# Mixture-of-experts stage on one Trainium2 core: two experts per matrix product on row halves, scaling on GpSimd, halves added by TensorE

## The reference, cut to what matters

```python
shared = jnp.zeros_like(h)
for s in range(shared_w.shape[0]):          # two shared experts
    shared = shared + _gelu(_c1(feats, shared_w[s], shared_b[s])) / shared_w.shape[0]
...
vals, idx = jax.lax.top_k(scores, TOP_K)    # TOP_K = 4
wts = jax.nn.softmax(vals / TEMPERATURE, axis=1)
gate_w = jnp.zeros((B, NUM_EXPERTS), x.dtype).at[jnp.arange(B)[:, None], idx].add(wts)
out = shared
for e in range(NUM_EXPERTS):
    out = out + _gelu(_c1(feats, expert_w[e], expert_b[e])) * gate_w[:, e][:, None, None, None]
return out + residual
```

## Time and profile before

| | us |
|---|---|
| median of 3 runs (lowest, highest) | 7360.36 (7358.43, 7375.71) |
| the profiled execution, its own time | 7338.2 |
| its span in the trace | 7336.4 |
| PE busy over the span | 6420.7 (88%) |
| DVE busy | 5526.3 (75%) |
| ACT busy | 3980.0 (54%) |
| POOL busy | 3924.6 (53%) |

### The profile page before, as it was taken

The page is one execution under the profiler, slowest core; times in us unless marked ns, Lnnn a source line. Parts: engine busy times, 40 slices in busy tenths (PEclk is TensorE's granted clock), DMA queues, the critical chain, the costliest instruction groups (busy, mean ns, idle before and its releaser), DMA issues. The chain is left out here.

```text
span 7336.4 us, 119069 instructions
## 1 busy us (share of the span) xinstructions
PE 6420.7 (88%) x36560; PEld 3370.5 (46%) x36560; DVE 5526.3 (75%) x5048; ACT 3980.0 (54%) x6930; POOL 3924.6 (53%) x2716
## 2 busy tenths in 40 slices
PE   8968699999987369876999999999989999999991
PEld 7852233333345224565222222222247777777771
DVE  4654577777732358401899999999979999999996
ACT  5425366666631357401666767767645555555552
POOL 0100122222210300000899999999979999999991
PEclk9989799999988689857999999999979999999995
DMA  2243233343345623444222222222220000000006
GB/s 72 71 163 143 59 99 97 99 101 99 100 119 125 249 103 103 128 104 73 39 41 38 39 40 37 40 40 37 34 63 11 10 9 9 10 10 9 9 7 187
DMA packets 638484, 518.35 MB, mean 71 GB/s; under 512 B 250045, under 2 KB 569315, under 8 KB 629627
## 3 DMA queue, kind: packets, MB, share of 16 engines
q1 hardware_dynamic: 636667, 507.10, 28.0%
q10 hardware_dynamic: 1600, 8.52, 0.5%
HBM read 304.91 MB, written 171.32 MB: 65 GB/s over the span
## 5 line engine op out<-in xcount | busy, mean ns | idle before, releaser
L2605 DVE TENSOR_TENSOR_SCAN spa_hs<-spa_p_d,spa_hs,spa_bx 128x967 f32<-128x967 f32 x584 | 1346.5, 2306 | 1.2 <-ACT spa_p_d L2504 1.1
L2311 POOL TENSOR_TENSOR spa_hc<-spa_hs,spa_cr 128x966 f32<-128x966 f32 x592 | 1313.8, 2239 | 44.4 <-DVE spa_hs L2605 40.2
L2759 POOL TENSOR_TENSOR spe_hc<-spe_hs,spe_bcu 128x1024 f32<-128x1024 f32 x520 | 1218.2, 2359 | 67.2 <-DVE spe_hs L2971 66.2
L2971 DVE TENSOR_TENSOR_SCAN spe_hs<-spe_p_d,spe_bx 128x1024 f32<-128x1024 f32 x520 | 1161.6, 2276 | 36.3 <-ACT spe_p_d L2919 33.0
L2846 PEld LDWEIGHTS spe_p_y<-spe_idt,spe_hc 128*128 128x128 f32 x8320 | 966.1, 192 | 143.8 <-issue 143.8
L1065 DVE TENSOR_REDUCE attention_nm<-attention_p_s 128x2 f32<-128x640 f32 x1024 | 789.1, 812 | 260.1 <-PE attention_p_s L922 259.0
L2846 PE MATMUL spe_p_y<-spe_idt,spe_hc 128*128 128x128 f32 x8320 | 979.2, 276 | 0.0
L1023 ACT ACTIVATE attention_pr<-attention_p_t 128x512 f32<-128x512 f32 x1280 | 712.0, 600 | 419.4 <-PE attention_p_t L945 287.2
L2504 ACT ACTIVATE spa_p_d<-spa_p_d,spa_av 128x483 f32<-128x483 f32 x1184 | 706.5, 636 | 376.3 <-PE spa_p_d L2375 376.3
L2919 ACT ACTIVATE spe_p_d<-spe_p_d 128x896 f32<-128x896 f32 x520 | 446.2, 902 | 758.7 <-PE spe_p_d L2829 758.4
L2375 PE MATMUL spa_p_d<-spa_du,spa_hot 32*128 32x483 f32 x2368 | 644.9, 620 | 12.8 <-DVE spa_hs L2605 3.3
(11 more groups left out here) (429 smaller groups left out, 10585.3 us busy)
## 6 DMA issues: line engine op xcount, KB each, us to landing
attention_qs<-scratch_qp SPq DMA_DIRECT2D x768, 64.0 KB, 2.8
spa_uc<-spa_du SPq DMA_DIRECT2D x148, 241.5 KB
attention_rc<-scratch_den SPq DMA_DIRECT2D x128, 256.0 KB
scratch_qp<-patch_parts SPq DMA_DIRECT2D x64, 384.0 KB, 2.3
spa_xt<-scratch_x SPq DMA_DIRECT2D x148, 121.5 KB, 2.7
front_xs<-in_x_dram SPq DMA_DIRECT2D x64, 256.0 KB, 3.0
scratch_xf<-front_out SPq DMA_DIRECT2D x128, 128.0 KB, 2.5
patch_x<-scratch_xf SPq DMA_DIRECT2D x8, 2048.0 KB, 18.8
```

What stands on the lines that cost most here:

```text
L2311: nc.gpsimd.tensor_tensor(hc[:, k % 8:k % 8 + 2, :], hs[:, k:k + 2, 0:NA], cr2[:, s % 2, :].unsqueeze(1).broadcast_to([128, 2, NA]), ALU.m ...
L2605: last = nc.vector.tensor_tensor_scan(joined(hs, j), p_d[j % 2][:, 511 - NA:512 + NA], joined(bx, j), hs[:, k, NA - 1:NA], ALU.mult, ALU.add)
L2759: nc.gpsimd.tensor_tensor(hc[:, k, :, d, :].rearrange("p s d t -> p d s t"), hs[:, k % 2, d, :, :], rows, ALU.mult)\
L2971: nc.vector.tensor_tensor_scan(hs[:, k % 2, d].rearrange("p d s t -> p (d s t)"), p_d[h][:, :], bx[:, k % 2, d].rearrange("p d s t -> p (d ...
```

## The change

What it does:

- **Products.** A product's weights are no longer 128 x 128 with two zero blocks. Two experts of one image stand side by side, 64 rows by 128 columns, and the product reads the 64 partitions of that image alone. So a chunk has three pairs k = 0, 1, 2 (first two chosen experts, the shared two, last two chosen), each of two products p = 0, 1 on the lower and upper row half, into banks `p_x[k][p]`: six banks. In a bank, partitions 0 to 63 hold one expert and 64 to 127 the other, all of one image. For that the shared weights `sw` and biases `sb` are laid out anew by the host.
- **Shared experts** (pair 1) are made one chunk ahead of the others. ACT writes their Gelu to SBUF (`gs`) and POOL multiplies by one half (`us`).
- **Sums.** DVE's `add_first` adds gate times pair 0 to `us` (into `acc`), `add_last` adds gate times pair 2. Then PE adds the two partition halves of `acc` with a 128 x 64 matrix `fold` of two identities (`add_halves`), images on different columns, into one of two banks `p_o`, and DVE's `finish` adds the residual.
- **Order.** The queues are written with `stream`, a helper that was there before: each part has a lag in chunks, so at step i the part with lag 1 works on chunk i - 1.
- **Building the weights.** Every second chosen expert's product with the selection is made by POOL; the reductions, now over all 128 partitions at once, stay on DVE: eight instead of sixteen.
- **Transfers.** 13 instead of 14 before the stream; `hot2` and `gx` gather every other expert's row. Four buffers for features instead of two. Chunks alternate between the two pairs of images.

The diff, cut (declarations, and the functions removed, which are shown above, are left out):

```diff
-def experts(nc, hr, feats, sel, wts, we, be, ws, bs, out1):
+def experts(nc, hr, feats, sel, wts, we, be, ws, bs, ident, out1):
...
+        def columns(s, r):
+
+            return bass.ds((r * 2 + s // 2) * 512, 512)
 
         @block.sync
...
+            with nc.allow_non_contiguous_dma(reason="every other expert's gate"):
+                for q in range(2):
                     r = slice(64 * q, 64 * q + 64)
...
+                    sp.dma_start(hot2[r], sel.rearrange("b (k q) e -> q (b k) e", q=2)[q:q + 1].broadcast_to([64, B * TOP // 2, NE]))\
+                        .then_inc(loaded, 16)
+                    sp.dma_start(gx[r].rearrange("p b k -> p (b k)"),
+                                 wts.rearrange("b (k q) -> q (b k)", q=2)[q:q + 1].broadcast_to([64, B * TOP // 2])).then_inc(loaded, 16)
+
+            def load(c, s, r):
+
+                after(sp, x_done, 4 * (c - 3))
+                sp.dma_start(fs[:, s, :], feats[:, s % 2, columns(s, r)]).then_inc(f_in[s], 16)
+
+            def store(c, s, r):
+                sp.wait_ge(out_ready, c + 1)
+                sp.dma_start(ov[:, s % 2, columns(s, r)], os[:, s % 2, :]).then_inc(stored[s % 2], 16)
+
+            stream(sp, NCH, UX, 2 * UX, 5, (0, load), (5, store))
...
+        @block.tensor
+        def _(pe):
+            def spread_shared(c, s, r):
+                pe.wait_ge(f_in[s], 16 * r + 16)
+                for p in range(2):
+
+                    after(pe, shared_active, 2 * c + (p - 1))
+                    rows = slice(64 * p, 64 * p + 64)
+                    nc.tensor.matmul(p_x[1][p][:, :], wsh[rows, :], fs[rows, s, :], start=True, stop=True).then_inc(shared_done, 1)
+
+            def spread(k, free):
+
+                def run(c, s, r):
+                    for p in range(2):
+
+                        after(pe, free, 2 * c + (p - 1))
+                        rows = slice(64 * p, 64 * p + 64)
+                        nc.tensor.matmul(p_x[k][p][:, :], wx[rows, s % 2, k // 2, :], fs[rows, s, :], start=True, stop=True).then_inc(x_done, 1)
+                return run
+
+            def add_halves(c, s, r):
+                after(pe, out_ready, c - 1)
+                for p in range(2):
+                    pe.wait_ge(last_added, 2 * c + (p + 1))
+                    mm = nc.tensor.matmul(p_o[s % 2][64 * p:64 * p + 64, :], fold[:, :], acc[:, s % 2, p, :], start=True, stop=True)
+                mm.then_inc(folded, 1)
...
+            stream(pe, NCH, UX, UX, 2, (1, spread(0, first_added)), (0, spread_shared), (1, spread(2, last_added)), (2, add_halves))
 
         @block.scalar
         def _(act):
...
+            stream(act, NCH, UX, UX, 1, (1, activate(0, first_active)), (0, activate_shared), (1, activate(2, last_active)))
 
         @block.vector
         def _(dve):
...
+            def choose(a, k, t):
+                nc.vector.tensor_reduce(wx[:, a, k // 2, C * (k % 2):C * (k % 2) + C], pk[:, t], AX.X, ALU.add).then_inc(w_ready, 1)
...
+            def add_first(c, s, r):
+                t, b = s % 2, lambda p: 2 * (s % 2) + p
+                for p in range(2):
+                    dve.wait_ge(first_active, 2 * c + (p + 1))
+                    dve.wait_ge(shared_scaled, 2 * c + (p + 1))
+
+                    after(dve, folded, c - 1)
+                    nc.vector.scalar_tensor_tensor(acc[:, t, p, :], p_x[0][p][:, :], gx[:, b(p), 0:1], us[:, t, p, :], ALU.mult,
+                                                   ALU.add).then_inc(first_added, 1)
+
+            def add_last(c, s, r):
+                t, b = s % 2, lambda p: 2 * (s % 2) + p
+                for p in range(2):
+                    dve.wait_ge(last_active, 2 * c + (p + 1))
+                    dve.wait_ge(first_added, 2 * c + (p + 1))
+                    nc.vector.scalar_tensor_tensor(acc[:, t, p, :], p_x[2][p][:, :], gx[:, b(p), 1:2], acc[:, t, p, :], ALU.mult,
+                                                   ALU.add).then_inc(last_added, 1)
+
+            def finish(c, s, r):
+                dve.wait_ge(folded, c + 1)
+
+                after(dve, stored[s % 2], 16 * (r * 2 + s // 2))
+                nc.vector.tensor_tensor(os[:, s % 2, :], p_o[s % 2][:, :], hr[:, s % 2, columns(s, r)], ALU.add).then_inc(out_ready, 1)
+
+            stream(dve, NCH, UX, UX, 2, (1, add_first), (2, finish), (1, add_last))
+
+        @block.gpsimd
+        def _(pool):
+            def scale(c, s, r):
+                for p in range(2):
+                    pool.wait_ge(shared_active, 2 * c + (p + 1))
+
+                    after(pool, first_added, 2 * c + (p - 3))
+                    nc.gpsimd.tensor_tensor(us[:, s % 2, p, :], gs[:, s % 2, p, :], share[:, :], ALU.mult).then_inc(shared_scaled, 1)
...
+            stream(pool, NCH, UX, UX, 0, (0, scale))
```

More of the change, by code:

```diff
@@ L66, in turns, with after, stream, fixed @@
     return run
+def after(eng, sem, n):
+    if not (isinstance(n, int) and n <= 0):
+        eng.wait_ge(sem, n)
+def stream(eng, n, unroll, head, tail, *parts):
+    def fixed(i):
+        for lag, part in parts:
+            c = i - lag
+            if 0 <= c < n:
+                part(c, c % unroll, c // unroll)
+    for i in range(head):
+        fixed(i)
+    with eng.Fori(0, (n - head) // unroll - 1) as j:
+        for s in range(unroll):
+            for lag, part in parts:
+                c = head + s - lag
+                part(j * unroll + c, c % unroll, j + c // unroll)
+    for i in range(n - unroll, n + tail):
+        fixed(i)
 KH = H // 2
@@ new lines, in experts @@
+        gx = st.sb("gx", [128, B, TOP // 2])
+        idt = st.sb("idt", [128, 128])
+        fold = st.sb("fold", [128, C])
+        share = st.sb("share", [128, 512])
+        fs = st.sb("fs", [128, UX, 512])
+        gs = st.sb("gs", [128, 2, 2, 512])
+        us = st.sb("us", [128, 2, 2, 512])
+        acc = st.sb("acc", [128, 2, 2, 512])
+        os = st.sb("os", [128, 2, 512])
+        p_x = [[st.ps(f"p_x{k}{p}", [128, 512]) for p in range(2)] for k in range(NP)]
+        p_o = [st.ps(f"p_o{s}", [128, 512]) for s in range(2)]
@@ L1885, in _, with activate_shared @@
-        @block.tensor
-        def _(pe):
-            pe.wait_ge(w_ready, 1)
-            for a in range(2):
-                @turns(pe, N)
-                def _(j):
-                    for s in range(2):
-                        n = a * N * 2 + 2 * j + s
-                        pe.wait_ge(f_in[s], 16 * (a * N + j) + 16)
-                        for k in range(NX):
-                            pe.wait_ge(summed[k], n)
-                            mm = nc.tensor.matmul(p_x[k][:, :], wx[:, a, k, :], fs[:, s, :], start=True, stop=True)
-                            mm.then_inc(x_done, 1)
+            def activate_shared(c, s, r):
+                for p in range(2):
+                    act.wait_ge(shared_done, 2 * c + (p + 1))
+                    after(act, shared_scaled, 2 * c + (p - 3))
+                    nc.scalar.activation(gs[:, s % 2, p, :], p_x[1][p][:, :], ACT.Gelu, bias=bsh[:, 0:1]).then_inc(shared_active, 1)
@@ L2081 @@
 TD = TK * DE
-def after(eng, sem, n):
-    if not (isinstance(n, int) and n <= 0):
-        eng.wait_ge(sem, n)
 RA = 7
```

160 lines of the change are left out of this document (57 added, 103 removed).

## The result

| | before | after |
|---|---|---|
| median, us (lowest, highest) | 7359.4 (7355.06, 7375.71) | 7414.78 (7405.14, 7419.34) |
| ratio of after to before, 95% interval | | 1.0069 [1.0053, 1.0085] |
| the profiled execution | 7338.2 | 7405.14 |

The account below looks back on a forecast made before the run. The prediction took TensorE to bound the experts stream, VectorE alone the weight building before it. Terms of -15.0, +1.0, +4.5 and -46.0 sum to -55.5, making 7338.2 into 7282.7; carried to the median, 7305 us, range 7275 to 7350.

Parts of the forecast that it names:

- Sum: -15.0 + 1.0 + 4.5 - 46.0: Whole kernel: weight building, loads, VectorE-GpSimd turn-taking and stream together give -55.5 us on the profiled 7338.2.
- Pairs at the same time (1.00 us a group): TensorE in the stream: both 64-row halves of a pair overlap, so every group costs 1.00 us, 4.0 per chunk.
- Rival 1: TensorE in the stream: pairs don't overlap, 6.9 us per chunk, 159 us more, 7464 us; chance 0.06.
- the dear end of its bounds: TensorE's array-shape changes: 0.28 us more per chunk, 18 in all; a late second half adds another 28.
- The ring: Stream, once per chunk: last add, third pair, folds, `finish` and two adds wait on each other, 4.4 us; chance 0.68.
- Rival 4: Stream: no cycle of waits sets the pace, TensorE's 4.0 us per chunk remains, 7279 us; chance 0.10.
- the 3.98 charged: ScalarE in the stream: six activations per chunk at 0.664 us each, 3.98 us.
- The stream, 289.4: Experts stage, 64 chunks at 4.4 us plus 7.8 of filling: 289.4 us against 335.4, a gain of 46.0.
- rivals 2 and 5: Stream: clock falls to 1.2 GHz, 7497 us, chance 0.03; or GpSimd and VectorE take turns, 7423 us, chance 0.02.
- Rival 3: Stream: waits and shape changes cost more, 4.65 to 5.1 us per chunk, 7323 to 7351 us; chance 0.11.
- Building, 15.9 + 4.5 = 20.4: Weights before the stream: 15.9 us against 30.9, plus 4.5 for VectorE and GpSimd taking turns, VectorE first.
- The loads, +1.0 (0 to 5): Transfers before the stream: four gathering every other row cost more issue time, with landing 1.0 us more.

Follow-up runs that it names:

- kernel 2: The changed kernel with 49 more TensorE instruction slots (waits on a semaphore) in the experts stage: 7322.56 us, ratio 0.9934 to the kernel before.
- kernel 3: The changed kernel with 49 more TensorE slots and VectorE's `finish` put behind the last add: 7290.49 us, ratio 0.9901 to the kernel before.

## Why the prediction was wrong, point by point

- **The step that failed** is the sum's last one: it changed four terms and carried the rest of the program over as it was ("Sum: -15.0 + 1.0 + 4.5 - 46.0", taken from 7338.2). The rest took 95 us more in the spectral stage, since the longer stream moved that stage's loop onto an eighth block. None of the five rivals held this. With the loop 12 or more instructions further on, the sign is as forecast (0.9934 in kernel 2, 41 us by medians, 49 by the ratio; forecast 55).
- **Pairs at the same time (1.00 us a group): right,** 1.02 to 1.13. Rival 1 (7464) did not happen. The drain at a change of tiling mode, which the Trainium skill states (TensorEngine Tiling (Array Packing), Key Properties), raised no group by more than 0.1 us: 1.13 for the pair behind the folds (2840.09), 1.02 for the pair behind a pair. The prediction had read the dear end of its bounds out of that rule; it did not come.
- **The ring, 4.4 us: right in its size and its parts.** Moving `finish` (kernel 3) showed that the ring sets the pace. Rival 4 put the pace without it at 4.0; it is 3.85. TensorE's groups follow each other by 0.96 to 1.01 us (2839.08, 2840.09, 2841.05), and ScalarE's six activations take 3.55 us, not the 3.98 charged.
- **The stream, 289.4: measured 287.5.** Granted clock 1.00 and scale-and-adds at 742 ns, so rivals 2 and 5 did not happen. (Rival 3's prices are 1 to 2 us too high by its own terms: 0.25 and 0.7 us a chunk give 7321 and 7350.)
- **Building, 15.9 + 4.5 = 20.4: measured 20.3,** with the turns as named: a GpSimd product takes 3.25 instead of 2.38 us. Yet I had not asked what VectorE alone would take. It is 20.1, so this edit brought nothing.
- **The loads, +1.0 (0 to 5): wrong, +9.8,** outside its bounds. I priced a strided transfer by its issue alone. The issue was cheap (0.64 us each), the landing was not: 5.3 and 9.5 us for transfers of 32 and 2 KB.
- **The difference between the profiled execution and the median:** carried over as 22 us. In all later kernels the second inverse transform, an unchanged stage ahead of the scans, takes 116 to 136 us between the first and last of its stores, also in the four that are the kernel before but for slots (127 to 131). In the profile before it took 111. Its stretch there, and then in the profile after:

```profile
3327.00:3438.00 111.00, 94.71 (x783) 85.44 (x781) 22.71 (x31) 17.95 (x30) 0.00 (x0) 0.92 0.59 86
```
```profile
3279.00:3408.00 129.00, 116.16 (x784) 105.16 (x783) 22.68 (x31) 17.91 (x30) 0.00 (x0) 0.75 0.54 74
```

  The granted clock was 0.92 in one and 0.75 in the other, for the same work. This is the 18 us of the table's fourth row, and most of the 22 us by which that execution lay under its median. What makes the clock differ there from execution to execution stays open.

## What to carry to other kernels

When an edit changes how many instructions an engine's queue holds, look at the loops behind it: their length and their place in blocks of 256, and the `q8 instruction` row before and after. This loop of 6.26 blocks ran free while it touched seven, and a dozen instructions that have nothing to do with it decided between seven and eight. A slower kernel whose edited stage got faster calls for a table by stage before any theory on the edit. And price a transfer by its landing where an engine waits for it, the more so when its elements are a few bytes apart.

## What the runs showed of the hardware that was not expected

- TensorE ran a loop of 1603 instructions over seven blocks of 256 without one fetch, and over eight blocks with some nine fetches for each of the 12 jumps back, 107 more in the whole program. So it does not read again the one block that is missing, but about all of them. The price was 42 or 95 us in 1779. The jump back took 3.6 to 3.7 us instead of 0.2, and with two instructions between its target and the next block's border another 3.05 us followed. The granted clock was at its lower level (0.50) for the 5 us after such a gap.
- The gathers of every other gate and selection row landed after 9.5 and 5.3 us; plain transfers with twice the bytes took 2.3 and 2.5.
- VectorE and GpSimd, both multiplying from SBUF, took turns down to the instruction: 2.43 us for a product that takes 0.28 alone.
